# Layer 3 of a four-layer stack: level products and placings issued in pairs, with four decayed buffers and three crossing buffers

## What is computed

```python
diff = cum[:, :, :, None, :] - cum[:, :, None, :, :]
Lmat = jnp.exp(jnp.where(tril, diff, -jnp.inf))
CB = jnp.einsum('bcihn,bcjhn->bcijh', Cc, Bc)
M = CB * Lmat * dtc[:, :, None, :, :]
Yd = jnp.einsum('bcijh,bcjhp->bcihp', M, xs_c)
...
y = (Yd + Yoff).reshape(Bsz, L, H, P) + D[None, None, :, None] * xs
yz = y * (z * jax.nn.sigmoid(z))
yn = yz * rsqrt(mean(yz * yz) + EPS) * norm_w      # then @ W_out.T
hidden = jax.nn.sigmoid(x1) * x2                   # the feed-forward beside it
```

## Time and profile before

| quantity | value |
|---|---|
| median of 3 runs | 1033.42 us (1028.28 to 1034.17) |
| the profiled execution | 1029.84 us |
| its span in the trace | 1028.0 us, so 1.84 us lie outside the span |
| PE busy over the span | 946.4 us (92%) |
| DVE busy | 715.1 us (70%) |
| ACT busy | 464.8 us (45%) |
| POOL busy | 435.2 us (42%) |

### The profile page before, as it was taken

The page is one execution under the profiler, slowest core; times in us unless marked ns, Lnnn a source line. Parts: engine busy times, 40 slices in busy tenths (PEclk is TensorE's granted clock), DMA queues, the critical chain, the costliest instruction groups (busy, mean ns, idle before and its releaser), DMA issues. The chain is left out here.

```text
span 1028.0 us, 12619 instructions
## 1 busy us (share of the span) xinstructions
PE 946.4 (92%) x4494; PEld 481.0 (47%) x4498; DVE 715.1 (70%) x1327; ACT 464.8 (45%) x767; POOL 435.2 (42%) x444
## 2 busy tenths in 40 slices
PE   4999799879999999878999997999999999999997
PEld 2677555323333333344555646633662474256325
DVE  3777565678888888547777773768586777758674
ACT  2333045247766666645575451621371246134411
POOL 2222357554444333017245361087128505840770
PEclk9999799979999999998999997999999999999999
DMA  8700035312211220030000001000000000000000
GB/s 295 259 16 16 16 105 141 123 40 65 63 47 49 63 63 2 1 146 1 17 16 1 16 1 44 1 0 1 21 1 1 1 21 1 0 1 22 0 1 21
DMA packets 28942, 43.67 MB, mean 42 GB/s; under 512 B 6512, under 2 KB 22080, under 8 KB 28480
## 3 DMA queue, kind: packets, MB, share of 16 engines
q1 hardware_dynamic: 28880, 42.87, 13.4%
HBM read 31.38 MB, written 11.27 MB: 41 GB/s over the span
## 5 line engine op out<-in xcount | busy, mean ns | idle before, releaser
L2180 POOL TENSOR_TENSOR l_scaled<-l_X,l_source 128x512 f32<-128x512 f32 x112 | 135.6, 1240 | 141.6 <-ACT l_X L2250 124.6
L1102 DVE TENSOR_REDUCE l_nmax<-banks 128x1 f32<-128x512 f32 (+1 forms) x165 | 147.7, 929 | 34.9 <-PE banks L1211 33.7
L1057 ACT ACTIVATE l1b_PT<-banks 128x512 f32<-128x512 f32 (+1 forms) x176 | 134.1, 793 | 66.8 <-PE banks L1224 66.4
L1211 PE MATMUL banks<-l_KQ 96*128 96x512 bf16 x240 | 81.3, 392 | 8.6 <-DVE l_nmax L1102 5.8
L1224 PE MATMUL banks<-l_KQ 99*128 99x512 bf16 x256 | 85.0, 385 | 3.0 <-ACT l1b_PT L1057 2.1
L2263 ACT ACTIVATE l_hhi<-l_h 128x512 f16<-128x512 f32 (+1 forms) x24 | 15.1, 630 | 129.4 <-DVE l_h L2375 129.4
L2599 PE MATMUL banks<-l_scaled,l_cbm 128*64 128x512 f32 x224 | 59.5, 613 | 10.7 <-POOL l_scaled L2180 10.6
L1238 PE MATMUL banks<-l1b_PT,l1b_V 128*32 128x512 f32 x512 | 68.2, 605 | 0.0
L2349 DVE TENSOR_TENSOR l_decayed<-banks,l_right_decay 128x512 f32<-128x512 f32 x56 | 38.4, 686 | 37.9 <-PE banks L2599 37.9
L2621 PE MATMUL banks<-l_decayed,w_place 64*128 64x512 f32 x224 | 63.2, 641 | 0.0
L1783 PE MATMUL banks<-l_xhi,l_ternary 128*128 128x512 f16 x128 | 49.8, 389 | 8.6 <-DVE l_h L1713 8.6
(11 more groups left out here) (342 smaller groups left out, 2052.1 us busy)
## 6 DMA issues: line engine op xcount, KB each, us to landing
l_split<-l1a_parts SPq DMA_DIRECT2D x16, 384.0 KB, 3.3
l_KQ<-l_split SPq DMA_DIRECT2D x48, 128.0 KB, 2.9
l_KQ<-l_split SPq DMA_DIRECT2D x16, 192.0 KB, 3.1
l_KQ<-l_split SPq DMA_DIRECT2D x48, 64.0 KB, 2.8
w_ternary<-l_tern_out SPq DMA_DIRECT2D x7, 384.0 KB, 2.3
x<-in_x SPq DMA_DIRECT2D x4, 512.0 KB, 9.4
l_raw<-in_w_gate_up SPq DMA_DIRECT2D x2, 1024.0 KB, 9.9
out<-x SPq DMA_DIRECT2D x4, 512.0 KB, 3.0
```

The lines of the kernel that those rows point to most:

```text
L1057: nc.scalar.activation(PT[:, first:first + size, :], source, ACT.Exp, scale=SCALE).then_inc(p_ready, 1)
L1102: nc.vector.tensor_reduce(nmax[:, H % 2, first:first + size], source, axis=AX.X, op=ALU.max, negate=True).then_inc(smax_read, 1)
L1211: last = nc.tensor.matmul(ps[bank + m][:, :], KQ[pairs, QUERY, g, j, t * P:(t + 1) * P], KQ[pairs, KEY, g, j, :], start=True, stop=True)
L2180: nc.gpsimd.tensor_tensor(by_head(scaled[:, (2 * u + m) % 4, :]), by_head(X[:, T, :]), spread(source[:, level, T, :]), ALU.mult).then_inc( ...
```

## The change

PE issues two products, then the placings of the two products before them, then at most one hidden tile. The hidden tiles move from behind products 4 and 10 to behind the placings that follow products 5 and 11, and all of them now come behind the placings. `decayed` gets a fourth buffer. `across` has three buffers where it had four: the fourth tensor reuses the first buffer, for which POOL waits until product 7 is made. DVE's list is put in the new order. No instruction is added or taken away. The core of the diff:

```diff
-    HIDDEN_AT = (-1, 1, 4, 7, 10, 13)
+    HIDDEN_AT = (-1, 1, 5, 7, 11, 13)
...
-        decayed = sb("decayed", [P, 3, INNER])
+        decayed = sb("decayed", [P, 4, INNER])
...
-        across = sb("across", [P, len(ACROSS), INNER])
+        across = sb("across", [P, len(ACROSS) - 1, INNER])
...
+                    if i == len(ACROSS) - 1:
+                        pool.wait_ge(prod_made, b * NI + (LEVELS + 1))
...
-                        if u >= 3:
-                            dve.wait_ge(placed, b * OWN + (u - 2))
+                        if u >= 4:
+                            dve.wait_ge(placed, b * OWN + (u - 3))
...
                 take_decayed(0)
+                take_decayed(1)
                 gated(0)
-                take_decayed(1)
...
-                for n in range(NI + 2):
+                for n in range(0, NI + 2, 2):
                     if n < NI:
                         product(n)
-                        if n == 0:
-                            pe.wait_ge(xtok_ready, b * TT + TT)
-                        for j in range(1, FT):
-                            if HIDDEN_AT[j] == n:
-                                hidden(b, j)
-                    if n >= 2 and ITEMS[n - 2][2] is None:
-                        place(n - 2)
+                        product(n + 1)
+                    if n == 0:
+                        pe.wait_ge(xtok_ready, b * TT + TT)
+                    for done in (n - 2, n - 1):
+                        if done >= 0 and ITEMS[done][2] is None:
+                            place(done)
+                    for j in range(1, FT):
+                        if HIDDEN_AT[j] == n + 1:
+                            hidden(b, j)
```

More of the change, by code:

```diff
@@ L2167, in scale_across @@
                     src, level = ACROSS[i]
-                    nc.gpsimd.tensor_tensor(by_head(across[:, i, :]), by_head(X[:, src, :]),
+                    if i == len(ACROSS) - 1:
+                        pool.wait_ge(prod_made, b * NI + (LEVELS + 1))
+                    nc.gpsimd.tensor_tensor(by_head(across[:, i % (len(ACROSS) - 1), :]), by_head(X[:, src, :]),
                                             spread(source[:, level, src, :]), ALU.mult).then_inc(across_ready, 1)
@@ L2346, in take_decayed @@
                             dve.wait_ge(decay_ready, b * 3 + 3)
-                        if u >= 3:
-                            dve.wait_ge(placed, b * OWN + (u - 2))
-                        nc.vector.tensor_tensor(by_head(decayed[:, u % 3, :]), by_head(bank),
+                        if u >= 4:
+                            dve.wait_ge(placed, b * OWN + (u - 3))
+                        nc.vector.tensor_tensor(by_head(decayed[:, u % 4, :]), by_head(bank),
                                                 spread(right_decay[:, level, pair, :]), ALU.mult).then_inc(bank_read, 1)
@@ L2421, in _ @@
                  .then_inc(coef_ready, 1))
-                take_decayed(2)
                 dve.wait_ge(coef_ready, b + 1)
                 start(0)
+                take_decayed(2)
                 take_decayed(3)
@@ L2427, in _ @@
                 rest_of_gated(0)
+                start(1)
                 take_decayed(4)
-                start(1)
                 take_decayed(5)
@@ L2432, in _ @@
                 statistics(0)
+                statistics(1)
                 take_decayed(6)
+                take_decayed(7)
                 gated(2)
-                statistics(1)
-                take_decayed(7)
                 take_decayed(8)
-                rest_of_gated(2)
                 take_decayed(9)
@@ L2441, in _ @@
                 take_placed(1, 7)
+                rest_of_gated(2)
                 gated(3)
                 take_decayed(10)
+                take_decayed(11)
                 weigh(0)
-                take_decayed(11)
                 weigh(1)
@@ L2448, in _ @@
                 take_decayed(12)
+                take_decayed(13)
                 gated(4)
                 start(2)
-                take_decayed(13)
                 start(3)
                 rest_of_gated(4)
+                take_decayed(14)
+                take_decayed(15)
                 statistics(2)
-                take_decayed(14)
                 statistics(3)
                 variance()
-                take_decayed(15)
                 gated(5)
@@ L2604, in product @@
                         for i in sources:
-                            last = nc.tensor.matmul(bank, cb[:, ACROSS[i][0], T * P:(T + 1) * P], across[:, i, :],
+                            last = nc.tensor.matmul(bank, cb[:, ACROSS[i][0], T * P:(T + 1) * P], across[:, i % (len(ACROSS) - 1), :],
                                                     start=(i == sources[0]), stop=(i == sources[-1]))
@@ L2620, in place @@
                         rows = slice(m * RIGHT, (m + 1) * RIGHT)
-                        last = nc.tensor.matmul(ps[6 + m][:, :], w.place[rows, level, :], decayed[rows, u % 3, :],
+                        last = nc.tensor.matmul(ps[6 + m][:, :], w.place[rows, level, :], decayed[rows, u % 4, :],
                                                 start=(level == 0), stop=(level == LEVELS - 1))
                     last.then_inc(placed, 1)
-                for n in range(NI + 2):
+                for n in range(0, NI + 2, 2):
                     if n < NI:
                         product(n)
-                        if n == 0:
-                            pe.wait_ge(xtok_ready, b * TT + TT)
-                        for j in range(1, FT):
-                            if HIDDEN_AT[j] == n:
-                                hidden(b, j)
-                    if n >= 2 and ITEMS[n - 2][2] is None:
-                        place(n - 2)
+                        product(n + 1)
[7 more added lines that the diff above has]
+                            hidden(b, j)
                 pe.wait_ge(h_ready, b * FT + FT)
```

## The result

The changed kernel takes 1052.02 us (median of 6 runs, 1050.14 to 1055.94), the kernel before 1033.8 in the same measurement. By the medians it is 18.2 us slower; the ratio is 1.0208, 95% interval 1.0183 to 1.0233. The profiled execution has a span of 1049.1 us, 21.1 more than the 1028.0 of before. All of it lies in the last layer: from the first level product to the last item's turning of y the trace has 363.9 us, before 342.7.

The account below looks back on a forecast made before the run. It took PE and POOL, feeding each other, as the bound. Stretch 11.2 us plus end stalls 5.1 gave 16.3: 1046 from the profiled 1029.84, 1049.7 from the median; forecast 1048, range 1037 to 1055.

Parts of the forecast that it names:

- The walk: Start times followed through PE's list from product 2 to the down matmuls, with POOL's waits: +2.8 us an item.
- The gain of 1.8 an item: Fewer runs of products, placings and hidden tiles on PE save 1.8 us an item, if PE is what bounds.
- The stall in front of hidden tile 5: At down, PE waits for DVE's `rest_of_gated(5)`, held by POOL's last normalise: 1.6 us in three items, 0.3 in the last.
- +10.4 - 8.87: From product 15's start: `rest_of_gated(5)` done at +10.4, hidden tile 5's down matmuls due at +8.87; stall taken as 1.6 us.
- The open question: Whether DVE's `rest_of_gated(5)` waits out POOL's 1.89 us instruction: stall 1.6 us if so, 0.3 if not; 1.6 taken.
- the third (+22): POOL falls further behind through paired SBUF-only DVE instructions, and the end stalls by 2.4 us: 1051 to 1056, chance 0.10.
- Rival 1: The stretch slows, but the end doesn't stall on `rest_of_gated(5)`: 1042 to 1046 us, chance 0.22.
- Rival 2: PE bounds, fewer switches pay: 1023 to 1026 us, chance 0.06; with all POOL waits gone 1012 to 1015, chance 0.03.

Follow-up runs that it names:

- e4: Changed kernel with four hidden tiles each put between the two products of a pair, and variance ahead of product 15 on DVE: 1029.17 us, ratio to before 0.9992.
- e1: Changed kernel's buffers kept, but PE and DVE in the order of the kernel before: 1031.65 us, ratio to before 0.9991.
- e11: Kernel before with POOL writing only heads 0 to 7 of the scaled and across rows: 1016.81 us, stretch 43.45 us.
- e12: Changed kernel with POOL writing only heads 0 to 7 of the scaled and across rows: 1014.5 us, stretch 41.62 us.
- e2: Changed kernel with the last two statistics and variance ahead of taking product 15 on DVE: 1055.41 us, ratio to before 1.0207.
- e9: Changed order on PE and DVE with the old buffers, three of `decayed` and four of `across`: 1045.78 us, one execution.
- e3: Changed kernel with six extra matmuls on PE ahead of products 5 and 11: 1050.61 us, ratio to before 1.0173.
- e10: Changed kernel with both the extra matmuls ahead of products 5 and 11 and variance ahead of product 15: 1046.52 us, ratio to before 1.0167.
- e8: Changed kernel's buffers with new PE and DVE orders worked out from measured durations: 1009.04 us, ratio to before 0.9813.

## Why the prediction came out as it did

**What held.** The bound was read right: PE and POOL feed each other, and what decides is what PE has to do while POOL writes. The walk's mechanism is shown by e4 (a hidden tile between the products takes away the stretch's whole loss) and e1 (in the old order the buffers do nothing). PE's waits for POOL, forecast at 7 to 8 us an item, are 7.1 at full clock, and POOL's behind P6 and P8, forecast at 1.4 and 3.8, are 1.49 and 3.71. Forecast +2.8 us an item for the stretch, measured 49.66 - 46.66 = +3.0 at full clock. The gain of 1.8 an item by fewer changes of tiling is there, but only where PE doesn't wait (e11, e12: 1.83). The stall in front of hidden tile 5 came as forecast and by the mechanism forecast: 1.4 us in three items (forecast 1.6, though its own +10.4 - 8.87 is 1.53) and 0.3 in the last; e2 took it away by moving POOL's instruction. The open question, whether DVE waits for the end of a long POOL instruction as of a short one, is settled for this one: L2383 lasted 1.80 us, until 0.5 after L2161's end. That agrees with the Trainium skill ("SBUF — State Buffer", section "SBUF: two separate sides"), by which the lock is held for the whole instruction.

**What failed: the sum, by a term that it lacked.** It read "11.2 + 5.1 = 16.3", for the stretch and the end, and had no term for PE's clock. Measured are 4 x 3.0 = 12.0 for the stretch, 3 x 1.4 + 0.3 = 4.5 for the end, and 4.8 of half clock, 21.3 together, against 21.1 by the spans. The two terms that it had come to 16.5, so nearly all of what was missing is the 4.8. The walk had PE idle for 1.5, 2.3 and 2.7 us at a time and priced every matmul behind these gaps at the pace of before, where the clock was 1.00 throughout the stretch. It named the gaps and didn't ask what they do to the clock. The rival that came nearest to the size, the third (+22), did so by other causes: at full clock the stretch grew by 3.0, not by 3.7, and down took 1.4 more, not 2.4.

**Rival 1** (no stall) fell by the rows at 722.09 and 723.95. **Rival 2** (the switches pay) fell on the real kernel and is what e12 shows with POOL taken out of the way.

**Also wrong, in small.** The fourth buffer of `decayed` was priced at 0 us, because "it removes a wait that the new order would make": it does remove a wait, and the kernel with the old buffers has a stretch 0.85 us shorter (e9). And the forecast of 1048 was set below the 1049.7 that the sum gave from the median of the runs; the sum from the median would have been nearer to 1052.02. The sum comes nearer to the medians' difference (18.2) than to the spans' (21.1), but that is luck: the medians also hold the 5 us by which whole executions vary.

## What to carry to other kernels

In a list that an engine executes in order, pairing two instructions to save a switch puts the second one's wait ahead of all that stood between them: price what used to cover that wait before pricing the switch, and put work that is ready (here the hidden tile) into the gap. Where two engines feed each other, walk both lists with durations from rows; up to the first half clock it gave every start listed here within 0.11 us, and it also shows where to move things. And when a walk says that PE will idle for some microseconds, add a term for the clock.

## What the runs showed of the hardware that was not expected

- PE's clock fell to half inside a dense stretch whose longest idle time was 2.54 us. The first time it was at 0.50 from 702.3 to 705.7 us, after PE had idled 0.43 us ahead of 697.19 and 2.54 ahead of 700.80. It doesn't happen in every item, nor alike in e2 and the changed kernel (8.4 and 4.8 us in all, for the same gaps). Six matmuls in each of two gaps an item ended it in all four items (e3, e10).
- A DVE instruction on SBUF only waits for the end of a long POOL instruction too: 1.80 us for one of 0.68, beside a POOL instruction of 1.89.
- One placing takes 1.06 us, two in a row 1.91 (678.14 to 680.05), three in a row 2.78 (e8, 675.67 to 678.45): each further one of the same tiling adds about 0.86, so a run costs about 0.20 on top, and by the same working 0.15 for products (128 rows by 64 columns). Nine runs fewer gave 1.83 us (e11, e12).
